# Layer 1 attention: exponentials taken head by head from the score banks, and the halves of the probabilities transposed by one DMA a tile

## What is computed

```python
# layer 1 attention, for each of 64 batches: x (256, 256), context (77, 256), 16 heads of 64
q = layernorm(x) @ Wq * 64 ** -0.5
k, v = ctx @ Wk, ctx @ Wv
weights = softmax(q @ k.T)              # a head: 256 x 77
x = x + tanh(g) * (weights @ v) @ Wo    # then the feed-forward part of layer 1 on x
```

## Time and profile before

| | |
|---|---|
| median of the runs | 3129.29 us |
| profiled execution, span | 3124.2 us |
| layer 1 loop | about 1530 us to 3110 us of the span |
| TensorE busy | 2797.3 us, 90% |
| VectorE busy | 2640.9 us, 85% |
| GpSimd busy | 2190.1 us, 70% |
| ScalarE busy | 1875.0 us, 60% |

### The profile page before, as it was taken

How to read it: one execution, slowest core, us unless ns; L and a number is a source line. 1 busy time by engine, 2 the same in 40 slices (tenths; PEclk the granted TensorE clock), 3 DMA queues, 4 the chain that set the end, 5 groups by cost and what they waited for, 6 DMA issues and landing times.

```text
span 3124.2 us, 101333 instructions
## 1 busy us (share of the span) xinstructions
PE 2797.3 (90%) x33450; PEld 2225.3 (71%) x33450; DVE 2640.9 (85%) x6703; ACT 1875.0 (60%) x3733; POOL 2190.1 (70%) x3924
## 2 busy tenths in 40 slices
PE   4889896788888888869899999999999999999997
PEld 2444444666666666647688888888888888888886
DVE  6887886888888888875699999998989988999986
ACT  2666765777777777775455545555545555555553
POOL 3892001666667666645488888888888888888887
PEclk9999998999999999989999999999999999999999
DMA  5987666232223222623444444444444344444441
GB/s 153 361 332 289 244 243 227 73 86 79 73 78 83 80 74 77 224 82 81 96 104 111 107 101 95 104 104 95 101 91 97 94 103 104 96 98 93 108 94 43
DMA packets 367621, 388.79 MB, mean 124 GB/s; under 512 B 118432, under 2 KB 341264, under 8 KB 362320
## 3 DMA queue, kind: packets, MB, share of 16 engines
q1 hardware_dynamic: 346960, 335.42, 38.9%
q0 software_dynamic: 7328, 23.40, 2.4%
q10 hardware_dynamic: 12960, 25.23, 2.2%
HBM read 235.08 MB, written 148.83 MB: 123 GB/s over the span
## 4 chain that ended last, share of the span: by engine, by line
PE 39%; DVE 6%; issue 3%; POOL 2%; ACT 2%; DVEq 0%; POOLq 0%; ACTq 0%
PE banks L150 11%; PE banks L152 11%; PE banks L151 10%; PE banks L1310 2%; PE banks L1295 2%; DVE a_probT_lo L1397 1%; PE banks L1342 1%; ACT a_qT_hi L1199 1%; DVE a_pick L1522 1%; DVE a_y L1541 1%; DVE a_rsum L1409 1%; PE banks L1365 1%; DVE a_wsel L1531 0%; PE banks L1357 0%; ACT a_ynT_hi L1199 0%
## 5 line engine op out<-in xcount | busy, mean ns | idle before, releaser
L1199 ACT ACTIVATE a_qT_hi<-banks 128x512 f16<-128x512 f32 x252 | 150.5, 597 | 700.8 <-PE banks L152 700.8
L383 POOL TENSOR_TENSOR a_probT_lo<-a_expT,a_probT_hi 128x512 f16<-128x512 f32 (+1 forms) x384 | 372.0, 998 | 243.7 <-ACT a_probT_hi L458 243.7
L449 ACT ACTIVATE a_expT<-banks,a_top,w_score_scale 128x512 f32<-128x512 f32 (+1 forms) x384 | 272.2, 709 | 111.4 <-PE banks L544 111.2
L1112 POOL TENSOR_TENSOR a_pn<-a_prob,a_rsum 128x1024 f32<-128x1024 f32 (+1 forms) x256 | 307.2, 1221 | 5.8 <-DVE a_rsum L1411 5.3
L150 PE MATMUL banks<-a_xnT_hi,w_q_hi 128*128 128x256 f16 x1024 | 281.6, 275 | 4.7 <-DVE a_xnT_lo L1395 3.0
L150 PE MATMUL banks<-a_vo_front,a_probT_hi 128*128 128x256 f16 x1024 | 278.9, 272 | 2.7 <-DVE a_probT_lo L1397 2.6
L152 PE MATMUL banks<-a_xnT_hi,w_q_lo 128*128 128x256 f16 x1024 | 280.9, 274 | 0.0
L151 PE MATMUL banks<-a_xnT_lo,w_q_hi 128*128 128x256 f16 x1024 | 280.9, 274 | 0.0
L152 PE MATMUL banks<-a_vo_front,a_probT_lo 128*128 128x256 f16 x1024 | 279.0, 273 | 0.0
L151 PE MATMUL banks<-a_vo_front,a_probT_hi 128*128 128x256 f16 x1024 | 279.0, 272 | 0.0
L1397 DVE SCALAR_TENSOR_TENSOR a_probT_lo<-banks,a_probT_hi 128x512 f16<-128x512 f32 (+1 forms) x384 | 212.6, 582 | 35.7 <-ACT a_probT_hi L1199 35.3
(11 more groups left out here) (400 smaller groups left out, 10655.0 us busy)
## 6 DMA issues: line engine op xcount, KB each, us to landing
vo<-kv_vo_out SPq DMA_DIRECT2D x38, 2048.0 KB, 7.6
a_vo_front<-vo SPq DMA_DIRECT2D x128, 512.0 KB
kt<-kv_k_out ACTq DMA_DIRECT2D x9, 2560.0 KB, 15.0
a_k<-kt SPq DMA_DIRECT2D x64, 308.0 KB, 3.5
kv_raw_e<-in_L_ffn_w POOLq DMA_DIRECT2D x16, 1024.0 KB, 9.7
a_x<-in_x SPq DMA_DIRECT2D x64, 256.0 KB
a_y<-in_x SPq DMA_DIRECT2D x64, 256.0 KB, 2.8
x<-a_y SPq DMA_DIRECT2D x64, 256.0 KB, 2.2
```

The costliest lines, as they stand in the source:

```text
L383: pool.tensor_tensor(probT[b][1][0:rows, first:end, :], expT[b][0:rows, first:end, :], probT[b][0][0:rows, first:end, :], ALU.subtract).th ...
L449: act.activation(expT[1 - h][0:rows, first:end, :], bank, ACT.Exp, bias=top[0:rows, 0:1], scale=weights["score_scale"][0:rows, 0:1]).then_ ...
L1112: last = pool.tensor_tensor(keys_of(pn[h]), keys_of(prob_of(u, h, 2)), rsum[h][:, :].unsqueeze(2).broadcast_to([P, H, n]), ALU.mult)
L1199: act.activation(out, bank[:, 0:cols].rearrange("p (c s) -> p c s", c=out.shape[1]), ACT.Copy, scale=scale)\
```

## The change

All of it lies in layer 1's attention:

- ScalarE takes the exponential from the score banks itself, one instruction a head (16 of 128x77), with the head's shift as bias and the score scale as scale, both read from SBUF. The four shifts of VectorE and the one exponential of 1232 columns go. TensorE's next `scores` waits for `exp_done`. The exponentials of tile t are made in iteration t, after the two `low` and before `wselT_hi`.
- VectorE forms the 16 shifts (`shift_amounts`), sums 1232 exponentials (`inverse_sums`, now in iteration t after `wsel`, and waiting for `exp_done` of the same tile), and multiplies them by the reciprocal (`normalise`, first in the next iteration, three instructions). GpSimd's sums and its product go.
- ScalarE makes the high half of `pn` (`high_part`, 128x1280 to float16), GpSimd the low half (`low_part`), side by side in `parts`.
- SyncE issues one `dma_start_transpose` a tile (128 x 2560 of float16 in SBUF, to 20 blocks of 128 x 128 in SBUF, four buffers) ahead of the store; the ten transposes on TensorE and the reads of their three banks go. `high_part` of a tile waits until the transpose of the tile two before has landed, and `attend` until its own has.
- The transposed `xnT` takes two banks of the ring in place of one.

The core of the diff (`turn_probabilities` and the first `body` are SyncE's, `low_part` GpSimd's, `exponentials`, `high_part` and the `body` after them ScalarE's, then one line of TensorE's `scores`, the rest VectorE's):

```diff
+        def turn_probabilities(t, p, n):
+            need(sp, prob_lo, t + 1)
+            sp.sem_inc(turn_begun, 1)
+            sp.dma_start_transpose(probT[n][:, :, :], parts[p][:, :, :].rearrange("p a n -> p (a n)")).then_inc(probT_in[n], 16)
         def body(i, u, j):
             if live(i + 1, NB):
                 load_keys(i + 1, *ahead(u, j, 1))
             for h in range(TPB):
+                if live(i * TPB + h - 2, NT):
+                    turn_probabilities(i * TPB + h - 2, h, turned_place(2, u, h, j)[0])
...
+        def low_part(t, p):
+            need(pool, y_ready, t - TURNED + 1)
+            need(pool, prob_hi, t + 1)
+            pool.tensor_tensor(parts[p][:, 1, :], pn[p][:, :], parts[p][:, 0, :], ALU.subtract).then_inc(prob_lo, 1)
...
+        def exponentials(t, p):
+            need(act, bias_ready, t + 1)
+            need(act, pn_ready, t - 1)
+            position = 0
+            for bank, held in enumerate(BANK_HEADS):
+                for slot in range(held):
+                    at = bank * BANK + slot * KEYS
+                    last = act.activation(prob[p][:, position, :], ps_scores[:, at:at + KEYS], ACT.Exp,
+                                          bias=shift_by[:, position:position + 1], scale=score_scale[:, 0:1])
+                    position += 1
+            last.then_inc(exp_done, 1)
+        def high_part(t, p, u, h, j):
+            turned, times = turned_place(3, u, h, j)
+            need(act, pn_ready, t + 1)
+            if live(t - 2, NT):
+                need(act, probT_in[turned], (times + 1) * 16)
+            act.activation(parts[p][:, 0, :], pn[p][:, :], ACT.Copy).then_inc(prob_hi, 1)
         def body(i, u, j):
...
                 prep(1)
+                if live(t - 1, NT):
+                    high_part(t - 1, 1 - h, u, h, j)
                 if live(t - 4, NT):
...
+                if live(t, NT):
+                    exponentials(t, h)
                 if live(t - 7, NT):
                     bank = full(i, ("wselT", h))
                     act.activation(wselT[:, :], bank[0:BIAS_ROWS, 0:P], ACT.Copy).then_inc(wselT_hi, 1)
...
-            need(pe, scores_read, t)
+            need(pe, exp_done, t)
...
+        def inverse_sums(t, p):
+            need(dve, exp_done, t + 1)
+            nc.vector.reduce_sum(rsum[p][:, :], prob[p][:, :, :], AX.X).then_inc(summed, 1)
+            need(dve, summed, t + 1)
+            nc.vector.reciprocal(rsum[p][:, :], rsum[p][:, :]).then_inc(recip_done, 1)
+        def normalise(t, p):
+            need(dve, recip_done, t + 1)
+            need(dve, prob_lo, t - 1)
+            nc.vector.scalar_tensor_tensor(out=first_keys(pn[p]), in0=prob[p][:, :, 0:FRONT], scalar=PROB_TOP,
+                                           in1=rsum[p][:, :].unsqueeze(2).broadcast_to([P, H, FRONT]),
+                                           op0=ALU.mult, op1=ALU.mult)
...
+                if live(t - 1, NT):
+                    normalise(t - 1, 1 - h)
+                prep(0)
                 prep(1)
                 if live(t, NT):
                     maximum(t)
+                    shift_amounts(t)
...
                         .then_inc(wsel_ready, 1)
+                if live(t, NT):
+                    inverse_sums(t, h)
                 if live(t - 5, NT):
                     nearest_two(t - 5, h)
```

More of the change, by code:

```diff
@@ L960, in prep_uses @@
     def prep_uses(h, part):
[L962 removed]
+        at = {(0, 1): [("xnT", c) for c in range(DC)], (0, 2): [("q", 0)], (0, 3): [("q", 1)], (1, 0): [("q", 2)], (1, 2): [("q", 3)]}
         return at.get((h, part), [])
@@ L1214, in body @@
                 prep = lambda part: prepare(i, (u + 1) % 2, h, part) if live(i + 1, NB) else None
[L1215 to L1220, removed]
-                    if g == 1 and live(t - 1, NT):
-                        need(act, scores_read, t)
-                        part = prob_of(u, h, 1)[:, :]
-                        act.activation(part, part, ACT.Exp, scale=score_scale[:, 0:1]).then_inc(exp_done, 1)
+                prep(0)
                 prep(1)
+                if live(t - 1, NT):
+                    high_part(t - 1, 1 - h, u, h, j)
                 if live(t - 4, NT):
@@ L1267, in prepare @@
                     need(pe, xn_ready, i + 2)
-                    bank = bank_for(i, use)
-                    for c in range(DC):
-                        for a in range(TPB):
-                            last = nc.tensor.transpose(bank[:, c * SEQ + a * P:c * SEQ + (a + 1) * P],
-                                                       xn[:, a, c * P:(c + 1) * P], ident[:, :])
+                    bank, c = bank_for(i, use), use[1]
+                    for a in range(TPB):
+                        last = nc.tensor.transpose(bank[:, a * P:(a + 1) * P], xn[:, a, c * P:(c + 1) * P], ident[:, :])
                 else:
-                    need(pe, xnT_ready, i + 2)
+                    need(pe, xnT_ready, (i + 2) * DC)
                     bank = bank_for(i, use)
@@ L1299, in scores @@
             last.then_inc(scores_full, 1)
-        def turn_probabilities(i, t, h, g):
-            need(pe, pn_ready, t + 1)
-            bank = bank_for(i, ("probT", h, g))
-            first, end = GROUPS[g]
-            rows = HEIGHT[g]
-            at = 0 if first < MAIN else MAIN * P
-            for c in range(end - first):
-                place = at + (first % MAIN + c) * rows
-                last = nc.tensor.transpose(bank[0:rows, c * P:(c + 1) * P], pn[1 - h][:, place:place + rows], ident[:, :])
-            filled(last, i, ("probT", h, g))
         def attend(i, t, h, u, j):
             p, before = turn(u, j, 2, h - 2)
-            need(pe, probT_ready, (t + 1) * PG)
+            turned, earlier = turned_place(3, u, h, j)
+            need(pe, probT_in[turned], (earlier + 1) * 16)
             need(pe, vo_in[p], (before + 1) * VALUE_LOADS)
@@ L1321, in attend @@
                 value = vo_front[p][:, c, :, :] if c < MAIN else vo_back[p][:, c - MAIN, :, :]
-                last = matmul3(nc, bank[:, 0:D], [x[0:rows, c, :] for x in probT], [value[:, k, :] for k in range(2)],
+                last = matmul3(nc, bank[:, 0:D], [probT[turned][0:rows, k * CHUNKS + c, :] for k in range(2)], [value[:, k, :] for k in range(2)],
                                c == 0, c == CHUNKS - 1)
@@ L1329, in body @@
                 prep = lambda part: prepare(i, (u + 1) % 2, h, part) if live(i + 1, NB) else None
-                for g in range(PG):
-                    if live(t - 3, NT):
-                        turn_probabilities(i, t - 3, h, g)
-                    if g == 0:
-                        prep(0)
-                    if g == 1 and live(t, NT):
-                        scores(i, t, h, u, j)
+                prep(0)
+                if live(t, NT):
+                    scores(i, t, h, u, j)
                 prep(1)
@@ L1417, in maximum, with shift_amounts @@
             nc.vector.reduce_max(third_max, third, AX.X).then_inc(max_done, 1)
[L1419 removed]
+        def shift_amounts(t):
             need(dve, max_done, t + 1)
[L1422 to L1431 removed]
+            nc.vector.tensor_scalar(shift_by[:, :], smax[:, :], score_scale[:, 0:1], -1.0, ALU.mult, ALU.mult)\
+                .then_inc(bias_ready, 1)
         def prototype_products(i, t, h):
```

132 lines of the change are left out of this document (46 added, 86 removed).

## The result

The changed kernel takes 3646.2 us (median of four runs, 3640.9 to 3648.6) against 3129.6 for the kernel before in the same session: 1.165 times as long (95% interval 1.164 to 1.167). The forecast was 3635 us, in a range of 3420 to 4010, slower with a chance of 0.95. The profiled execution's span is 3639.2 us, 515 more than the 3124.2 of before. First the busy times and two of the page's costliest groups, with the waits ahead of them; the columns are those of the earlier trace rows.

The account below looks back on a forecast made before the run. TensorE bounds the kernel before; after the change, a loop through SyncE's value loads and the DMA transpose was to set 32.5 us a batch against 24.5. 8.0 us over 63 batches, 504 us, gave 3635 us, range 3420 to 4010.

Parts of the forecast that it names:

- the second loop: SyncE's store and value loads, odd tile's transpose, ScalarE and VectorE up to the next store: 26.4 us + T a batch.
- T: Time of a DMA transpose from issue to landing, taken as 6.1 us for 640 KB, as a copy.
- the way from `high_part` to the store: ScalarE's 8.5 us, VectorE's part up to L1541 5.7 us, and hops between engines.
- The 12.0: SyncE's time from the store of h = 0 to the end of the eight value loads, 12.0 us.
- the first loop: ScalarE from `high_part` through exponentials to `wselT_hi`, then VectorE to the normalisation: 16.1 us a tile, 32.1 a batch.
- my 0.34: Pitch in us of one 77-column exponential on ScalarE; sixteen take 5.5 us a tile.
- the 2.7 us of `high_part` to `low`: ScalarE's work ahead of the exponentials, claimed to hide VectorE's maximum, which comes after the normalisation.
- Slow or blockwise transposes (1, 2): DMA transposes landing in 8 to 16 us, 3753 to 4257 us, chance 0.20; blocks singly, 4950 us, 0.05.
- Short exponentials (3): ScalarE's exponentials at a pitch of 0.2 us: 3488 us, or 3325 at T = 3; chance 0.10.
- Faster (4): TensorE stays the bound at 22.1 us a batch, both loops under 24.5: 2978 us, chance 0.03.
- The clock: TensorE, busy 68% of a batch, at 0.8 clock needs 27.6 us a batch, under the loop; nothing added.

Follow-up runs that it names:

- its experiment: The changed kernel with the 16 maxima kept in unused PSUM columns of a score bank instead of SBUF: 3548.7 us, ratio 1.137.
- the experiments with all levers: Changed kernel with three exponentials a tile, maxima in PSUM, values late, engines reordered: 3157.3 us; reordered further 3144.9; also without GpSimd's subtraction 3137.1.

## Why the prediction was right, and where its parts were not

**Sign, mechanism and size hold.** The waits that close a loop over ScalarE and VectorE were named with their place, and the trace and the experiments show them: fewer exponentials take 318 us off, and the exponentials by head with the sums and the normalisation on VectorE make the loss without the transposes. 8.0 us a batch were forecast, 515 / 63 = 8.2 came. That the time came within 11 us is in part luck: the number was taken from the loop that does not decide, and in the loop that does, two errors cancelled.

**Which loop decides was wrong, by little.** I had the second loop at 32.5 us a batch and the first at 32.1. Measured, the second comes to 12.04 (store to transpose, 2602.38 to 2614.42) + 5.5 (landing) + 13.72 (`high_part` at 2621.05 to the store at 2634.77) = 31.3, under the batch of 32.4. Two terms were too large: T, 5.5 for 6.1 us, and the way from `high_part` to the store, 13.7 for 8.5 + 5.7 + 0.2 = 14.4, where the sixteen exponentials took 0.7 less than their term. The 12.0 held. It agrees with this that moving the values alone changed nothing that the intervals can tell.

**Two errors in the first loop cancel.** Sixteen exponentials take 4.82 us to the start of the next instruction (2608.70 to 2613.52), a pitch of 0.30 for my 0.34, which is 2 x 0.7 = 1.4 us a batch too much. Missing was the hold of `shift_amounts`: 97 us by its experiment, 97 / 63 = 1.5 us a batch. Without the hold the kernel takes 3548.7 us, and the forecast would have been 86 us over. The step that failed is the one that said the maximum "is hidden by the 2.7 us of `high_part` to `low`": true of the maximum's own 1.5 us, but not with the 2.1 us of `shift_amounts` behind it. GpSimd's new subtraction was costed for GpSimd alone.

**Smaller terms** came as costed: `high_part` 1.27 us for 1.2, `low_part` 2.61 for 2.5, the sum 1.43, the pitch of the normalisation from 2619.45 to 2620.93, 1.48 for 1.53.

**The rivals.** Slow or blockwise transposes (1, 2) fall by T = 5.5. The Trainium skill's 1309 ns for a block (VectorE: DVE Perf Modes, The three transpose paths), one after another, would have been an estimated 26 us, and the trace, with 4.8 to 8.1 us for twenty blocks, does not agree. Nor did the prediction's estimate of 1.7 to 1.9 us for T come (1.6 to 1.9 when worked out again): the shortest landing took 4.8. Short exponentials (3) were closest, 0.30 instead of 0.34, far from the 0.2 it wanted. Faster (4) needed both loops under 24.5 us, which the changed kernel's are not. With both loops loosened, in the experiments with all levers, no kernel came under the one before either.

**The clock** was 0.95 from 2300 to 2500 us, with TensorE busy 75%; nothing was added for it and nothing was needed, since the loop that decides has none of TensorE's work in it. The prediction misread a row here: both slices of the earlier trace rows at 6 tenths busy have a clock of 8 tenths, and those at 7 keep 9.

## What to carry to other kernels

Before work is moved off the full engine, follow one iteration through the in-order engines and add up the durations round each loop of waits: a loop longer than the full engine's share sets the time, whatever the shares say. Splitting one long instruction into sixteen short ones costs the pitch of each; here 4.8 us for 1.3. When a long GpSimd operation is added, list VectorE's small operations of the kinds held here (`TENSOR_SCALAR` from SBUF, as the shift and the selections) that can start beside it, and cost them at up to the length of GpSimd's. Whether one starts just ahead of it or just behind decides: 0.23 or 2.1 us here.

## What the runs showed of the hardware that I had not expected

- A VectorE `TENSOR_SCALAR` of 16 columns from SBUF took up to 2.13 us when it started beside a GpSimd subtraction of 2.61 us, and 0.23 us with its input in PSUM or when it started ahead of the subtraction. Selections of 32 columns took 1218 ns in the mean in an order that puts them beside it, and 284 without it. `BATCH_NORM_STATS2` from SBUF was not held.
- GpSimd is held too. Its operation on one column, L1134, took 193 ns before the change (there L1146) and takes 549 in the mean now, the median still at 194; in the batch above it starts at 2602.95 with VectorE's normalisation (2602.93, 1.22 us) and ends just after it:

```profile
2602.95 1.25 POOL L1134 TENSOR_TENSOR a_dgap<-a_dist 128x1 f32<-128x1 f32 x1
```

- Issuing a DMA transpose of 128x2560 float16 values takes SyncE 2.96 us or more (2.96 and 3.71 us above), and it lands 5.5 us after its issue in the median, near the 6.1 that was estimated for a copy of its size from the earlier trace rows.
